# Sampling indices in three buffers and four parts, ScalarE's one-hots in mid-unit, and the mixer's weight work behind x's transposes

## The reference

```
x = x + deformable attention(group norm(x))                 # L0
x = x + relu(batch norm(conv3x3(group norm(x), w_mixed)))   # L1, w_mixed = attention-weighted kernels
t = t + causal attention(ln(t)); t = t + top-2 of 8 experts(ln(t))        # L2
t = t + linear attention(ln(t)); t = t + spectral mixer(ln(t))            # L3
```

```
def gather(iy, ix):
    idx = (jnp.clip(iy, 0, h - 1) * w + jnp.clip(ix, 0, w - 1)).astype(jnp.int32)
    g = jax.vmap(lambda f, i: jnp.take(f, i, axis=1))(flat, idx.reshape(b, -1))
    return g.reshape(b, cg, K2, h, w) * valid[:, None]
attn = jax.nn.softmax(jnp.einsum('bgnc,bgckn->bgnk', qf, ks_), axis=-1)
out = jnp.einsum('bgnk,bgckn->bgnc', attn, vs_)
```

## Time and profile before

| | |
|---|---|
| median of three runs | 235.49 us (235.47 to 236.01) |
| profiled execution | 237.68 us |
| its span | 235.9 us |
| busy: TensorE, VectorE, ScalarE, GpSimd | 85%, 72%, 46%, 16% of the span |
| granted TensorE clock, mean | 0.978 of full |
| the transfers of SP's queue | 15.86 MB, 22.2% of 16 engines' span |

### The profile page before, as it was taken

The page is one execution under the profiler, slowest core; times in us unless marked ns, Lnnn a source line. Parts: engine busy times, 40 slices in busy tenths (PEclk is TensorE's granted clock), DMA queues, the critical chain, the costliest instruction groups (busy, mean ns, idle before and its releaser), DMA issues.

```text
span 235.9 us, 6609 instructions
## 1 busy us (share of the span) xinstructions
PE 199.7 (85%) x2832; PEld 134.8 (57%) x2832; DVE 170.5 (72%) x389; ACT 107.6 (46%) x268; POOL 38.8 (16%) x54
## 2 busy tenths in 40 slices
PE   7899888999487978998788878759886987989995
PEld 2477488998487978643263444413323633545994
DVE  2699989689689889695784456689699859667101
ACT  2525986779666776432104270320499602046000
POOL 5923000043032133000002003114300000110000
PEclk9999999999997997999999999988999999999999
DMA  6550542552543520101132230000000080000000
GB/s 201 174 161 3 139 142 79 188 148 78 182 153 101 167 74 7 16 8 27 30 111 92 45 80 0 0 0 0 3 3 0 20 351 3 3 0 0 3 0 22
DMA packets 9389, 16.58 MB, mean 70 GB/s; under 512 B 3414, under 2 KB 5229, under 8 KB 9232
## 3 DMA queue, kind: packets, MB, share of 16 engines
q1 hardware_dynamic: 9216, 15.86, 22.2%
q10 hardware_dynamic: 144, 0.30, 0.3%
HBM read 15.38 MB, written 0.78 MB: 68 GB/s over the span
## 4 chain that ended last, share of the span: by engine, by line
DVE 33%; PE 31%; DMA 17%; ACT 8%; issue 5%; POOL 4%; POOLq 0%; SPq 0%; DVEq 0%
PE ps L1514 25%; DMA indexb<-index_rows 16%; POOL arena L573 2%; DVE arena L1408 2%; DVE arena L1405 2%; DVE onehot L1039 2%; ACT indexb L674 2%; PE ps L1801 2%; PE ps L1802 2%; DVE arena L442 1%; DMA cst<-in_cst 1%; POOL rstd L566 1%; DVE att L1091 1%; DVE comp L1372 1%; ACT indexb L629 1%
## 5 line engine op out<-in xcount | busy, mean ns | idle before, releaser
L1514 PE MATMUL ps<-table,onehot 128*128 128x64 bf16 x1728 | 54.7, 196 | 9.0 <-DVE onehot L1039 8.3
L1514 PEld LDWEIGHTS ps<-table,onehot 128*128 128x128 bf16 x1728 | 54.0, 100 | 10.5 <-ACT arena L689 7.4
L1514 PE MATMUL ps<-spare 128*128 128x512 bf16 (+1 forms) x187 | 51.1, 400 | 8.0 <-ACT onehot L629 2.7
L1514 PEld LDWEIGHTS ps<-spare 128*128 128x128 bf16 x187 | 16.7, 104 | 31.9 <-issue 4.6
L689 ACT ACTIVATE arena<-ps 128x512 f32<-128x512 f32 (+1 forms) x40 | 21.8, 550 | 17.6 <-PE ps L1514 17.2
L1039 DVE TENSOR_SCALAR onehot<-indexb,cst 128x2304 bf16<-128x2304 bf16 (+1 forms) x32 | 23.0, 748 | 6.9 <-DMA indexb<-index_rows 6.5
L1514 PE MATMUL ps<-arena 128*32 128x66 f32 (+5 forms) x380 | 22.7, 255 | 2.0 <-DVE arena L1408 1.5
L442 POOL TENSOR_TENSOR arena<-arena,w4p 128x288 f32<-128x288 f32 x18 | 13.9, 803 | 61.0 <-DVE arena L442 61.0
L1514 PEld LDWEIGHTS ps<-arena 128*32 128x32 f32 (+2 forms) x380 | 19.6, 136 | 4.9 <-DVE arena L1408 2.0
L566 POOL TENSOR_TENSOR rstd<-var_eps,cst 128x4 f32<-128x4 f32 (+2 forms) x9 | 8.8, 983 | 80.1 <-DVE var_eps L917 45.4
L629 ACT ACTIVATE indexb<-comp 128x128 bf16<-128x128 f32 x6 | 1.9, 309 | 27.9 <-DVE comp L929 27.9
(11 more groups left out here) (289 smaller groups left out, 338.7 us busy)
## 6 DMA issues: line engine op xcount, KB each, us to landing
indexb<-index_rows SPq DMA_DIRECT2D x21, 384.0 KB, 3.9
arena<-in_toep SPq DMA_DIRECT2D x1, 2120.5 KB, 8.2
l<-in_l SPq DMA_DIRECT2D x1, 646.5 KB
onehot<-lin_split SPq DMA_DIRECT2D x6, 96.0 KB
stu_fq<-in_stu SPq DMA_DIRECT2D x1, 560.0 KB, 3.8
table<-stu_split SPq DMA_DIRECT2D x7, 70.0 KB, 2.0
l<-in_l SPq DMA_DIRECT2D x1, 384.0 KB, 5.8
l<-in_l SPq DMA_DIRECT2D x1, 342.0 KB, 3.0
```

The costliest lines, as they stand in the source:

```text
L1514: return nc.tensor.matmul(out_ap, lhsT, rhs, start=start, stop=stop)
```

## The change

- A third index buffer: the unused last 2304 columns of `stu_fq` (whose first 1120 hold the mixer's weights), seen as bf16. Units go to buffers 0, 1, 2 by `u % 3`, each with its own semaphore; the waits for one-hots move from two units back to three.
- A unit's broadcast is in four parts of 9 rows (288 KB each) instead of three of 12 (384 KB). As before, from unit 2 on each part after the first waits for the one before.
- ScalarE makes its distances behind group 1 and its one-hots behind group 2, instead of 3 and 4.
- VectorE adds x2 ahead of `wpick` and `nwpick`. TensorE runs two fillers and x2's transposes ahead of the selection. "Mixer low" moves from ahead of ln's transposes to behind the values' product, ScalarE's last `split` behind its copies of the turned probabilities. TensorE now waits for the middle part's split ahead of the scores, since both use PSUM bank 6.

```
-        d_ix = (sem("index_loaded_even"), sem("index_loaded_odd"))
+        d_ix = tuple(sem(f"index_loaded_{i}") for i in range(3))
-        ixb = indexb[:].rearrange("p (u j n) -> p u j n", u=2, j=J)
+        ixb = [b.rearrange("p (j n) -> p j n", j=J) for b in (indexb[:, 0:J * P], indexb[:, J * P:], spare_index)]
+        PARTS = 4
+        index_parts = lambda u: PARTS * ((u + 2) // 3)
             for u in range(1, T):
-                if u >= 2:
-                    sp.wait_ge(s_oh, 2 * (u - 1))
                 if u >= 3:
-                    sp.wait_ge(s_oa, u - 2)
-                for third in range(3):
-                    if u > 1 and third:
-                        sp.wait_ge(d_ix[u % 2], 16 * (3 * ((u - 1) // 2) + third))
-                    js = slice(third * J // 3, (third + 1) * J // 3)
+                    sp.wait_ge(s_oh, 2 * (u - 2))
+                if u >= 4:
+                    sp.wait_ge(s_oa, u - 3)
+                for part in range(PARTS):
+                    if u > 1 and part:
+                        sp.wait_ge(d_ix[u % 3], 16 * (index_parts(u) - PARTS + part))
+                    js = slice(part * J // PARTS, (part + 1) * J // PARTS)
...
-                    if u + 1 < T and i == GRP - 2:
+                    if u + 1 < T and i == 1:
                         distances(u + 1)
-                    if u + 1 < T and i == GRP - 1:
+                    if u + 1 < T and i == 2:
                         own_one_hots(u + 1)
...
             split(stu3, 1, stu_ps, "sm", "s1")
-            split(stu3, 2, stu_ps, "sl", "s2")
...
                 copy(prob_t[:, b * 3 * P:(b + 1) * 3 * P], ps[:, b, 0:3 * P], a3, f"pt{b}")
+            split(stu3, 2, stu_ps, "sl", "s2")
...
+            dve.wait_ge(a2.sem, a2["y1"])
+            nv.tensor_tensor(out=x2, in0=x1[:], in1=y1, op=ALU.add).then_inc(v2.sem, v2.step("x2"))
             dve.wait_ge(vz.sem, vz["wcol"])
...
-            dve.wait_ge(a2.sem, a2["y1"])
-            nv.tensor_tensor(out=x2, in0=x1[:], in1=y1, op=ALU.add).then_inc(v2.sem, v2.step("x2"))
...
-            weights_prepared("selection")
+            occupied(2, 7)
             pe.wait_ge(v2.sem, v2["x2"])
...
             ins.then_inc(t2.sem, t2.step("x2T"))
+            weights_prepared("selection")
...
+            occupied_after(v3, ("eps", 2), bank=7)
             weights_prepared("mixer middle")
-            occupied_after(v3, ("eps", 2), bank=7)
-            weights_prepared("mixer low")
-            pe.wait_ge(aw.sem, aw["sl"])
...
             pe.wait_ge(a3.sem, a3["qc"])
+            pe.wait_ge(aw.sem, aw["sm"])
...
             ins.then_inc(t3.sem, t3.step("pv"))
+            weights_prepared("mixer low")
```

More of the change, by code:

```diff
@@ L126, in hybrid @@
         nwpick = sb("nwpick", [P, P])
-        stu, fq = stu_fq[:, 0:STU], stu_fq[:]
+        stu, fq, spare_index = stu_fq[:, 0:STU], stu_fq[:], stu_fq[:, 4096 - J * P // 2:].bitcast(BF16)
         c, f, p1, p2, p3 = columns(cst, CST), columns(front, FRONT), columns(l1, L1), columns(l2, L2), columns(l3, L3)
@@ L488, in _ @@
             for u in range(1, T):
-                if u >= 2:
-                    sp.wait_ge(s_oh, 2 * (u - 1))
                 if u >= 3:
-                    sp.wait_ge(s_oa, u - 2)
-                for third in range(3):
-                    if u > 1 and third:
-                        sp.wait_ge(d_ix[u % 2], 16 * (3 * ((u - 1) // 2) + third))
-                    js = slice(third * J // 3, (third + 1) * J // 3)
-                    sp.dma_start(ixb[:, u % 2, js, :].rearrange("p j n -> p (j n)"),
-                                 rows_d[u * J:(u + 1) * J, :][js].rearrange("j n -> (j n)").unsqueeze(0).broadcast_to([P, J // 3 * P]))\
-                        .then_inc(d_ix[u % 2], 16)
+                    sp.wait_ge(s_oh, 2 * (u - 2))
[5 more added lines that the diff above has]
+                    js = slice(part * J // PARTS, (part + 1) * J // PARTS)
+                    sp.dma_start(ixb[u % 3][:, js, :].rearrange("p j n -> p (j n)"),
+                                 rows_d[u * J:(u + 1) * J, :][js].rearrange("j n -> (j n)").unsqueeze(0).broadcast_to([P, J // PARTS * P]))\
+                        .then_inc(d_ix[u % 3], 16)
             def rows_first(ap):
@@ L673, in index_group @@
                 act.wait_ge(s_bc, i + 1)
-                nc.scalar.activation(ixb[:, 0, 4 * i:4 * i + 4, :].rearrange("p j n -> p (j n)"),
+                nc.scalar.activation(ixb[0][:, 4 * i:4 * i + 4, :].rearrange("p j n -> p (j n)"),
                                      ps[:, IB[i % 3], :], ACT.Copy).then_inc(s_bce, 1)
@@ L735, in distances @@
             def distances(u):
-                act.wait_ge(d_ix[u % 2], 48 * ((u + 1) // 2))
+                act.wait_ge(d_ix[u % 3], 16 * index_parts(u))
                 if u >= 2:
                     act.wait_ge(s_gp, groups(u - 2))
-                nc.scalar.activation(ohv[:, u % 2, 1, J - OWN:, :], ixb[:, u % 2, J - OWN:, :], ACT.Abs, bias=npidx[:])\
+                nc.scalar.activation(ohv[:, u % 2, 1, J - OWN:, :], ixb[u % 3][:, J - OWN:, :], ACT.Abs, bias=npidx[:])\
                     .then_inc(s_oa, 1)
@@ L1032, in one_hots @@
                 else:
-                    dve.wait_ge(d_ix[u % 2], 48 * ((u + 1) // 2))
+                    dve.wait_ge(d_ix[u % 3], 16 * index_parts(u))
                 if u >= 2 and half == 0:
@@ L1038, in one_hots @@
                         js = slice(js.start, J - OWN)
-                    ins = nv.tensor_scalar(ohv[:, u % 2, q, js, :], ixb[:, u % 2, js, :], c["pidx"][:, q:q + 1],
+                    ins = nv.tensor_scalar(ohv[:, u % 2, q, js, :], ixb[u % 3][:, js, :], c["pidx"][:, q:q + 1],
                                            None, ALU.is_equal)
```

## The result

The changed kernel took 252.63 us (median of four executions, 248.66 to 253.88), beside 235.75 us for the kernel before on the same chip: a ratio of 1.059 (95%: 1.050 to 1.068), so **slower by 5 to 7%**. Some executions of a kernel fall in a slower state, and every ratio here compares only the others of both kernels, so it is not the ratio of the medians. On the 235.49 us of the prediction the ratio gives 249.4 us (247.1 to 251.6). The forecast was 245.5, its range 239 to 251. The sign and the mechanism of the loads are as forecast, the size was put 4 us too low: the interval reaches past the range's upper end, and the plain median, 252.6, lies beyond it.

The account below looks back on a forecast made before the run. It took the sampling's queue of serial index loads as the bound. Four parts, with the third buffer's gain counted, gave +11.2 us and the mixer -1.2: +10.0 on 235.49, so 245.5 us, range 239 to 251.

Parts of the forecast that it names:

- The third buffer: Sampling: unit 2's first load no longer waits for unit 0's one-hots and lands at 32.0; gain 4.5 us, once.
- Four parts: Sampling loads: each 288 KB part takes 3.37 us alone, 4.1 in a pair; last load lands at 98.5, +11.2 us.
- Rivals 1: Sampling loads: a transfer's time follows its size, parts cost nothing extra, only the mixer's gain stays; 234.1 us, 11%.
- 2: Sampling: the loads stop binding and VectorE sets the pace at 7.7 us a unit; 227.7 us, 3%.
- 4: Sampling loads, half-way case: parts near 3 us; 239 us or a little under, 8%.
- ScalarE's passes: Sampling: moving ScalarE's two passes to groups 1 and 2 costs nothing as long as the load binds.
- TensorE takes the same 8.0 us: Sampling's last unit: after an idle stretch longer than 2 us, TensorE's matmuls take 8.0 us as before.
- Rival 3: Sampling's last unit: all 216 matmuls run at 1.2 GHz, not only the first 3 us; +4.1, 249.6 us, 10%.
- The mixer: Mixer stage: x2 and its transposes go ahead of the selection, so ln's transposes start 1.2 us earlier.
- inside the cover: Behind the values' product: the moved low-part matmuls stand among fillers at no price, 1 us if that cover were gone.
- rival 5: Mixer stage: its gain doesn't come through; 246.7 us, within the forecast's range, no chance given.

Follow-up runs that it names:

- the filler version: Changed kernel with three parts, the low part of the mixer's weights replacing five filler matmuls behind the scores: 229.95 us, ratio 0.974; again 231.3 us, 0.972.
- four parts with filler: Changed kernel, still four parts, with the low part of the mixer's weights replacing five filler matmuls behind the scores: 251.75 us, ratio 1.061.
- both with two parts: Kernel before with two parts, two buffers: 233.3 us, ratio 0.985; and the filler version with two parts instead of three: 232.4 us, 0.977.

## Why the prediction was right where it was, and where not

**The third buffer: right.** 32.27 for the first part of unit 2 (forecast 32.0). Its worth at the last load is 4.9 us with three parts (forecast 4.5), 2.1 with four (99.39 against 101.50).

**Four parts: right, a little small.** Forecast 3.37 us alone and 4.1 in a pair; the trace has means of 3.38 alone and 4.16 in the five pairs, and the last load at 99.4 instead of 98.5. The price of the fourth part is 17.0 us with three buffers (82.35 to 99.39), forecast 15.7 (11.2 + 4.5), and 14.2 with two (87.28 to 101.50). With two buffers the median time to landing is 3.2 us for 192 KB, 3.4 for 288, 3.7 to 3.9 for 384 and 4.3 for 576: three times the data cost 1.1 us. With three buffers the medians by buffer spread more: 3.5 to 3.9 for 288 KB, 3.5 to 4.2 for 384, 4.2 to 5.0 for 576. The Trainium skill, "DMA: Bandwidth & Descriptors", section on the anatomy of a DMA, has 2.0 us and bytes over 436 GB/s; for the two ends that is an estimate of 2.45 and 3.35 us. The trace agrees with the slope (0.9 against 1.1 us) and not with the fixed part: the two ends measured 0.75 and 0.95 us more on this queue, and the measured one decides. Rivals 1, 2 and 4 fall with this.

**ScalarE's passes: right as far as tested.** Priced at nothing as long as the load binds; put back in the three-part kernel, the last one-hots moved by 0.1 us. With four parts no run moved them alone, but four parts without them lost as much.

**"TensorE takes the same 8.0 us": nearly.** Behind an idle time of 4.09 us it took 8.62, +0.65. Rival 3 had +4.1 for all 216 matmuls at the lower level (12.1 us); that did not happen, though in unit 5 they took 9.01. Nor does the length of the gap give the price: in before, 3.10 us ahead of unit 4 cost nothing (6.46) and 1.91 ahead of unit 5 cost 1.5 (7.99); in six parts alone, gaps of 7.1 to 8.4 us were followed by 7.7 to 8.9. The prediction read its 8.0 from the two gaps with a fall and passed over the one without.

**The mixer: the gain was right, "inside the cover" was the step that failed.** The early start came (forecast 1.2, measured 1.13 at ln's transposes). I then let the low part's matmuls go under behind the values' product at no price, and at 1 us if that cover were gone. The cover is fine at full clock. At half clock it isn't: the low part and seventeen fillers fill the stretch without a gap, and what waits is no longer VectorE's result but TensorE's list. The distance from y1 to the experts, by trace:

| order of TensorE's work | clock stays at 1.00 | clock falls to 0.50 |
|---|---|---|
| before's | 28.76, 28.74, 28.75 (before; four parts alone; six parts) | 29.41 (two parts alone) |
| the change's | 27.62, 27.64 (no wait between parts; passes back) | 29.00, 29.14, 29.11, 29.00 (after; three parts twice; mixer alone) |
| low part as filler | none seen | 28.82, 28.29, 28.47, 28.48 |

So the change's order is worth 1.1 us where the clock stays and 0.3 to 0.4 where it falls. In the trace of after it fell, and set against before's trace, where it stayed, nothing was left of the gain at the experts (29.00 against 28.76): that is what rival 5 said, and the run with the mixer's part alone says the same (1.002). It fell in four of six traces of the change's order against one of four of before's. What sets the fall stays open. The same instructions stand there with both outcomes, so the order alone doesn't force it; nor are ten traces enough to say that the order makes it likelier. The two codes that were traced twice, three parts and the filler version, each fell both times, so chance between executions is not shown for this place either. In the trace of after, TensorE had been busy for 0.98 us in 150 to 152 and for all of 152 to 154, and then the clock fell; before's trace has the same two figures (138 to 140, 140 to 142) and no fall.

**What the sum left out: 1.6 us** in the key-value sums of the last block, which the change doesn't touch. The kernel with four parts alone has the old code there and shows the same:

```profile
195.89 3.38 PE L1514 MATMUL ps<-arena 128*32 128x66 f32 x128 [1.47 <-DVE arena L1408]
```

It isn't the code, though: of the fourteen traces eight took 3.3 to 3.7 us there (after, four parts alone, six parts alone, both three-part ones, the mixer alone, the first filler one, four parts with filler) and six took 2.05 (before, no wait between parts, passes back, the second filler one and both with two parts). The filler version had 3.55 in one trace and 2.05 in the other, so this place differs between executions of one kernel. The forecast was a difference on one profiled execution, and that one had the full clock there, where the trace of after had not: that is luck of the two traces. +0.65 and +1.6 are clock, +1.4 is the low part under the lower clock, and together they are most of the 4.5 us by which the span grew beyond the forecast's 10.0; the rest, 0.9, is the loads.

## What to carry to other kernels

Where transfers wait for each other, count round trips: one costs 3.2 us at 192 KB and 3.5 to 4.2 at 384, and each part more adds a round trip to every unit. More buffers can only remove the waits for buffers; read in the queue's waits how many of them ever came last (here one) before adding any. And a filler or a moved piece is covered only at the clock at which the cover was read: work it out at the lower level too, as what had 1 us of slack at 2.4 GHz had none at 1.2.

## What the runs showed of the hardware

- TensorE can stop for 0.9 to 2.7 us with no recorded wait, in mid-row of equal matmuls. In the sampling only three kernels had such stops, eight in all: the one with no wait between parts and both with two parts. They are those in which from unit 2 on 1152 KB can be in flight together, and from 36 us on they alone had windows of 2 us with 299 GB/s and up (the next kernel had 292); with three, four or six serial parts no stop was longer than 0.24 us. The rate alone is no rule: two of the eight stops had at most 286 GB/s over 2 us ahead of them, and up to 396 GB/s from 28 to 36 us, while the first loads run, brought none in any trace. The stops stand at the same instructions in different traces. They eat what larger or freer transfers win: 84.1 instead of 81 for the last one-hots, and 88.0 against 84.3 for the last unit's matmuls. Late instructions are the suspect, not shown.
- The granted clock behind the values' product differs between kernels with the same instructions there, and costs 1.5 us of distance (27.6 or 29.1) with the change's order, 0.65 (28.76 or 29.41) with before's. Elsewhere it differs between two executions of one kernel: the three-part one took 6.46 and 8.01 us for the last unit's matmuls, the filler version 3.55 and 2.05 for the key-value sums.
- The executions of one kernel spread by more than the forecast's 0.3%: before had 233.9 to 241.8 us over a batch, the three-part kernel 231.2 to 234.4. A difference under 1% needs both kernels in one batch.
